# Softmax sums over a key tile and a sum of two tiles that GpSimd adds

## The chip, the cores and the metric

One core of a Trainium2 chip runs the whole program. The metric is the device time of one execution in microseconds. The kernel before took 1427.5 us (median of 3 runs, 1418.71 to 1435.67).

## The reference

A small network over eight sequences of 384 tokens, 512 wide: a state-space layer makes 256 tokens of each, 128 text tokens follow, then comes attention, then a mixture of 64 experts (6 for each token) with a shared expert. The change is in the attention, which is, for 16 query heads and 4 key heads of 32:

```python
x = layernorm(h)
q, k, v = heads(x @ Wq.T), heads(x @ Wk.T), heads(x @ Wv.T)
q = q * cos + rotate_half(q) * sin
k = k * cos + rotate_half(k) * sin
attn = softmax(q @ k.T * 32 ** -0.5)
h = h + (attn @ v) @ Wo.T
```

and, behind it, each token's six experts and its place in each expert's list, which the kernel works out while later sequences are in the attention:

```python
scores = softmax(x2 @ gate_w.T)
topk_w, topk_i = top_k(scores, 6)
pos = place_in_expert_list(topk_i)
```

## The kernel before, in words

The program has three stages: the state-space layer, the attention with the routing, and the experts. The attention is a software pipeline over passes b = -1 to 7. Pass b has 16 slots, n = 0 to 15, one for each query head of sequence b. In them the engines also prepare sequence a = b + 1 (normalise, transpose, project, rotate, transpose the heads, row maxima of the raw scores), project the output of c = b - 1, normalise and route d = b - 2, and place e = b - 3. Five engines run five instruction streams in the order in which the program is written, tied by semaphores. Nothing reorders them, so an instruction that waits holds up all that stands behind it on its engine.

A slot of the matrix engine (TensorE, PE) begins with the head's scores (L912): three matmuls, transposed, so that keys are on the partitions and the three key tiles of 128 keys by 384 queries lie in three PSUM banks. ScalarE takes the exponential of all three at once (L1171) into PT, a ring of eight heads in SBUF. The sums of the softmax and the products with the values are made by `values` (L916), for a group of four heads that share a key head, one group behind: in slots 4 to 7 for heads 0 to 3, and so on, the last group in slots 0 to 3 of the next pass. A step is one key tile for four heads, four matmuls with 32 columns of weights side by side. There are six: q = 0, 1, 2 multiply by ones (the sums), q = 3, 4, 5 by the values. `VALUE_STEPS` deals them to the four slots of a group as 2, 2, 1, 1. VectorE inverts the sums in the third slot of the group (L1421 to L1423) and multiplies at its end (L1431).

What else stands around the change:
- In slots 1, 2 and 4 PE projects the queries of sequence a, in slots 2, 3 and 5 its keys and values (L903). VectorE rotates each tile a slot later (L1387 to L1389), and GpSimd adds the two halves of the rotation (L1654, `rope_sum`) in slots 3, 4 and 6, into r1.
- In slot 7 PE transposes the heads out of r1 (L984). The first of these waits for the last `rope_sum`. ScalarE copies a rounded high part to qhi (L1278), VectorE the rest to qlo (L1395).
- SyncE copies qhi and qlo into the stacked operand QT of the scores, by `stack`: twelve transfers for eight heads, counted by stacked[half]. The half for heads 0 to 7 goes out at the end of pass b, that for heads 8 to 15 at the start of pass b + 1, behind `store_sums` (L806), which waits for the residual that VectorE makes in slot 0. Four small transfers (`stack_max`, L774) add the row maxima, counted by the same semaphore.
- The routing of sequence e: VectorE makes one-hot rows and a mask in slot 3 (L1466 to L1475), PE counts places in slot 4 (L1039), VectorE adds bases (L1487 to L1489), GpSimd adds the slot numbers and multiplies (L1663, L1665, three L1669, `places`), VectorE reduces that in slot 6 (L1495, `slots`), ahead of its last rotation. GpSimd scatters the result by 18 small DMAs (L1682) in slots 8 to 15.
- In slots 0, 1 and 5 GpSimd makes the low part of finished outputs (L1658, `out_lo`).

SBUF is nearly full: qhi, qlo, r1 and the normalised, transposed rows xT are parts of one arena, each free only between its last reader in one pass and its writer in the next.

## Time and profile before

| what | value |
|---|---|
| runs | 1418.71, 1427.5, 1435.67 us |
| profiled execution | 1441.19 us |
| its span, first to last instruction | 1439.4 us |
| mean granted TensorE clock | 0.945 of full |
| TensorE matmul busy | 1247.1 us (87%) |
| VectorE, ScalarE, GpSimd busy | 747.1, 417.8, 503.2 us (52%, 29%, 35%) |

The profile is of one execution. Times are microseconds from its first instruction. A row of the timeline gives start, duration, engine, line, operation, output from inputs, and in brackets how long the engine sat idle before it and what ended that.
### The profile page before, as it was taken

What the parts mean: (1) busy time and instruction counts of PE and PEld (TensorE: products, weight loads), DVE (VectorE), ACT (ScalarE), POOL (GpSimd) and SP (SyncE); (2) the same over time, 40 slices, a digit from 0 to 9 for tenths busy, and PEclk for the clock granted to TensorE, in tenths of its full rate; (3) what the DMA queues carried; (4) which work ended last, traced back from release to release, by engine and by line L of the source; (5) the groups of instructions that cost most, each with busy time, mean ns of one, the idle gap of its engine ahead of it and who ended that gap; (6) DMA issues with size and microseconds to landing.
All of it is one profiled execution on the core that took longest, in us unless ns stands there. A gap on an engine that the chain in (4) does not pass through costs nothing. (4 is left out here: it accounts for less than half of the span.)

```text
span 1439.4 us, 23556 instructions
## 1 busy us (share of the span) xinstructions
PE 1247.1 (87%) x9192; PEld 798.8 (55%) x9192; DVE 747.1 (52%) x1667; ACT 417.8 (29%) x693; POOL 503.2 (35%) x453
## 2 busy tenths in 40 slices
PE   6263778889999999999898789999999999989995
PEld 5253534445555554546455778666666666656662
DVE  7994457666677878686864532332322223222221
ACT  2220314344445444445354411111111111111110
POOL 0000101111114444443557673334444543444444
PEclk9698669999999999999999889999999999999997
DMA  3024142312525251615165263999999999998983
GB/s 115 0 62 101 39 89 42 86 42 64 129 63 134 53 144 43 155 35 136 46 198 181 97 195 53 290 309 295 303 336 341 299 337 343 282 299 284 331 271 40
DMA packets 144310, 239.82 MB, mean 167 GB/s; under 512 B 64569, under 2 KB 84681, under 8 KB 144201
## 3 DMA queue, kind: packets, MB, share of 16 engines
q1 hardware_dynamic: 120360, 214.10, 46.7%
q0 software_dynamic: 23840, 24.23, 9.4%
q8 instruction: 73, 1.20, 0.4%
q14 instruction: 37, 0.30, 0.1%
HBM read 175.59 MB, written 38.90 MB: 149 GB/s over the span
## 5 line engine op out<-in xcount | busy, mean ns | idle before, releaser
L2063 POOL DMA_INDIRECT out_rows<-mo_y,mo_scatter_half x128 | 182.9, 1429 | 239.8 <-DMA out_rows<-mo_y,mo_scatter_half 152.2
L1404 DVE TENSOR_REDUCE at_maxes<-at_ps 128x1 f32<-128x384 f32 x384 | 196.3, 553 | 59.5 <-PE at_ps L947 51.6
L1171 ACT ACTIVATE bulk<-at_ps 128x1152 f32<-128x1152 f32 x128 | 144.5, 1129 | 252.8 <-PE at_ps L912 251.5
L1682 POOL DMA_INDIRECT slot_table<-at_toki,at_si x144 | 145.5, 1011 | 119.9 <-DVE at_maxes L1404 87.0
L70 PE MATMUL mo_ps<-arena_view,arena_view 128*117 128x384 f32 (+1 forms) x864 | 168.8, 344 | 1.1 <-PEq L570 1.1
L70 PEld LDWEIGHTS mo_ps<-arena_view,arena_view 128*117 128x117 f32 (+1 forms) x864 | 146.5, 179 | 14.6 <-issue 14.5
L947 PE MATMUL at_ps<-late_view,late_view 128*128 128x384 bf16 x384 | 117.5, 352 | 28.9 <-DVE at_maxes L1404 16.7
L903 PE MATMUL at_ps<-arena_view,arena_view 128*128 128x512 f32 (+1 forms) x576 | 114.9, 351 | 3.6 <-ACT arena_view L1256 2.1
L903 PEld LDWEIGHTS at_ps<-arena_view,arena_view 128*128 128x128 f32 x576 | 90.6, 193 | 36.1 <-issue 22.3
L947 PEld LDWEIGHTS at_ps<-late_view,late_view 128*128 128x128 bf16 x384 | 31.0, 98 | 138.5 <-DVE at_maxes L1404 103.0
L912 PE MATMUL at_ps<-arena_view 97*128 97x384 f32 x384 | 96.4, 360 | 8.3 <-DMA arena_view<-at_mrow 5.1
L2038 DVE SCALAR_TENSOR_TENSOR mo_hm<-mo_sil,mo_wcol,mo_ps 128x352 f32<-128x352 f32 x32 | 18.6, 580 | 159.7 <-ACT mo_sil L1962 138.7
L903 PE MATMUL at_ps<-late_view,late_view 128*128 128x512 f32 x288 | 92.1, 436 | 6.1 <-POOL late_view L1658 4.3
L1658 POOL TENSOR_TENSOR late_view<-arena_view,late_view 128x384 fp32r<-128x384 f32 x32 | 32.0, 1012 | 160.8 <-ACT late_view L1233 160.8
L1908 PE MATMUL mo_ps<-late_view,mo_xgT 128*64 128x352 f32 x512 | 81.8, 474 | 5.7 <-DVE mo_xgT L2031 5.7
L1654 POOL TENSOR_TENSOR arena_view<-arena_view,arena_view 128x640 f32<-128x640 f32 x24 | 37.3, 1555 | 137.9 <-DVE arena_view L1389 137.9
L931 PE MATMUL at_ps<-bulk,at_ones 128*32 128x384 f32 x768 | 83.3, 513 | 1.3 <-ACT bulk L1171 0.8
L78 PE MATMUL mo_ps<-arena_view,arena_view 117*128 117x512 f32 (+1 forms) x324 | 78.9, 397 | 4.8 <-DVE arena_view L1995 4.8
L931 PE MATMUL at_ps<-bulk,arena_view 128*32 128x384 f32 x768 | 81.7, 499 | 0.0
L912 PEld LDWEIGHTS at_ps<-arena_view 97*128 97x128 f32 x384 | 67.9, 193 | 23.3 <-ACT bulk L1171 7.9
L1908 PE MATMUL mo_ps<-bulk,mo_xgT 128*64 128x352 f32 x512 | 79.3, 462 | 0.0
L78 PEld LDWEIGHTS mo_ps<-arena_view,arena_view 117*128 117x128 f32 (+1 forms) x324 | 59.6, 188 | 20.8 <-ACT arena_view L1950 5.5
(222 smaller groups left out, 1771.8 us busy)
## 6 DMA issues: line engine op xcount, KB each, us to landing
bulk<-in_L_ffn_w_gate SPq DMA_DIRECT2D x32, 704.0 KB
bulk<-in_L_ffn_w_up SPq DMA_DIRECT2D x32, 704.0 KB
late_view<-in_L_ffn_w_gate SPq DMA_DIRECT2D x32, 704.0 KB
late_view<-in_L_ffn_w_up SPq DMA_DIRECT2D x32, 704.0 KB
arena_view<-arena_view SPq DMA_DIRECT2D x96, 192.0 KB
late_view<-in_L_ffn_w_down SPq DMA_DIRECT2D x32, 512.0 KB
bulk<-in_L_ffn_w_down SPq DMA_DIRECT2D x32, 512.0 KB
out_rows<-at_hr SPq DMA_DIRECT2D x8, 768.0 KB
```

Source lines behind the costliest of these rows:

```text
L70: m = T.matmul(out, self.gu[:, wa, g, k, self.SO[c]:self.SO[c] + self.SW[c]], self.x2[:, xa, k, :], start=(n == 0), stop=(n == last))
L78: m = T.matmul(out, self.h[0:self.SW[c], xa, c, s * P:(s + 1) * P], self.d[0:self.SW[c], wa, c, :], start=(n == 0), stop=(n == last))
L903: m = T.matmul(out, xs[:, xa, k, x_cols], ws[:, wa, k, w_cols], start=(n == 0), stop=(n == 3 * KC - 1))
L912: m = T.matmul(ps[:, kt, 0:SEQ], QT[:, NH + h // REP, kt * P:(kt + 1) * P], QT[:, h, :], start=True, stop=True)
L931: m = T.matmul(ps[HD * j:HD * (j + 1), 3 + sums, 0:SEQ], w, PT[:, (REP * G + j) % RING, kt, :], start=(kt == 0), stop=(kt == NT - 1))
L947: T.matmul(ps[:, raw_bank(a, u), 0:SEQ], qb[:, r, s * P:(s + 1) * P], kb[:, g, :], start=True, stop=True).then_inc(raw_scores, 1)
L1171: A.activation(PT[:, N % RING, :, :], ps[:, 0:NT, 0:SEQ], ACT.Exp, scale=float(HD) ** -0.5)\
L1404: V.tensor_reduce(maxes[:, half, s, h:h + 1], ps[:, raw_bank(a, u), 0:SEQ], AX.X, ALU.max, negate=True)\
L1654: G.tensor_tensor(r1[:, s], r1[:, s], r2[:, s % 2], ALU.add).then_inc(rope_add, 1)
L1682: G.indirect_dma_start(slot_table, bass.IndirectOffsetOnAxis(ap=si[:, e % 2, m:m + 1], axis=0), toki[:, e % 2, m // TOPK:m // TOPK + 1], N ...
L1908: m = M.matmul(ps[CAP * e:CAP * (e + 1), 1 + g, 0:I], xgT[:, k, CAP * e:CAP * (e + 1)], wgu[j][:, e, g, k, :], start=(k == 0), stop=(k == ...
L2063: G.indirect_dma_start(acc_halves, bass.IndirectOffsetOnAxis(ap=scatter_half[:, half, 2 * p + e:2 * p + e + 1], axis=0), y[:, p % 2, e, co ...
```

## The change

For the seven sequences b = 0 to 6 (28 groups) GpSimd adds the exponentials of key tiles 0 and 1 of each head, 128x384 f32, as soon as they are there (`add_pair_of_tiles`), and the matrix engine multiplies tile 2 and this sum by ones: two sum steps in place of three. The five steps are dealt to the slots of a group as 2, 1, 1, 1. The last sequence keeps six steps.

The sums of the pairs need room, and there is no free buffer: they lie over qlo (heads 0 to 3), the high half of xT (heads 4 to 7), its low half (heads 8 to 11) and r1 (heads 12 to 15). So the first addition of each four waits until what lies there has been read: the stack of heads 8 to 15, the last projections, or the transposes of the heads. The next writers of these buffers wait for the sums of that group. The row maxima get a semaphore of their own, so that GpSimd can wait for the stack alone.

```diff
@@ attention_phase, tables @@
+        max_stacked = [sem(f"max_stacked{i}") for i in range(2)]
+        pair_added = sem("pair_added")
...
-        VALUE_STEPS = {0: (0, 1), 1: (2, 3), 2: (4,), 3: (5,)}
+        VALUE_STEPS = {0: (0, 1), 1: (2,), 2: (3,), 3: (4,)}
+        LAST_STEPS = {0: (0, 1), 1: (2, 3), 2: (4,), 3: (5,)}
+        ADDED = NKV * (B - 1)
+
+        def sum_steps(G):
+            return NT - 1 if G < ADDED else NT
...
-        STACK = 16 * (2 * 6 + P // HD)
+        STACK = 16 * 2 * 6
+        MAX_STACK = 16 * (P // HD)
+        PAIR_SUM = [part(arena, (15872, 6144, 7680, 10752)[g], [REP, SEQ]) for g in range(NKV)]
@@ SyncE @@
-                                 .bitcast(F32), mrow[HD * j:HD * j + NH // 2, half, :, :]).then_inc(stacked[half], 16)
+                                 .bitcast(F32), mrow[HD * j:HD * j + NH // 2, half, :, :]).then_inc(max_stacked[half], 16)
...
+                sp.wait_ge(sums_done, NKV * (B - 1))
@@ TensorE @@
                 if h in (0, NH // 2):
                     pe.wait_ge(stacked[2 * h // NH], STACK * (b + 1))
+                    pe.wait_ge(max_stacked[2 * h // NH], MAX_STACK * (b + 1))
...
-                kt, sums = q % NT, 1 - q // NT
+                first = sum_steps(G)
+                kt, sums = (q, 1) if q < first else (q - first, 0)
+                if first < NT and sums:
+                    kt = NT - 1 - q
...
-                if q == NT:
+                if q == 1 and G < ADDED:
+                    pe.wait_ge(pair_added, REP * (G + 1))
+                if q == first:
...
-                    m = T.matmul(ps[HD * j:HD * (j + 1), 3 + sums, 0:SEQ], w, PT[:, (REP * G + j) % RING, kt, :],
-                                 start=(kt == 0), stop=(kt == NT - 1))
-                if q == NT - 1:
+                    added = q == 1 and G < ADDED
+                    probs = PAIR_SUM[g][:, j, :] if added else PT[:, (REP * G + j) % RING, kt, :]
+                    m = T.matmul(ps[HD * j:HD * (j + 1), 3 + sums, 0:SEQ], w, probs,
+                                 start=q in (0, first), stop=q in (first - 1, first + NT - 1))
+                if q == first - 1:
...
-                    G, steps = NKV * b + n // REP - 1, VALUE_STEPS[n % REP]
+                    G = NKV * b + n // REP - 1
+                    steps = (VALUE_STEPS if G < ADDED else LAST_STEPS)[n % REP]
@@ ScalarE @@
+                        wait(act, sums_done, NKV * (b - 1) + 3)
@@ VectorE: rope, q_lo, max_row @@
+                if s == 0:
+                    wait(dve, sums_done, NKV * (a - 1))
...
+                if i == 0 and a >= 1:
+                    dve.wait_ge(sums_done, NKV * (a - 1) + 1)
...
-                    dve.wait_ge(stacked[half], STACK * a)
+                    dve.wait_ge(max_stacked[half], MAX_STACK * a)
@@ GpSimd @@
+            def add_pair_of_tiles(b, n):
+                g, N = n // REP, NH * b + n
+                if n % REP == 0:
+                    if g == 0:
+                        pool.wait_ge(stacked[1], STACK * (b + 1))
+                    elif g in (1, 2):
+                        pool.wait_ge(q_ready, NT * (b + 2))
+                        pool.wait_ge(kv_ready, NT * (b + 2))
+                    else:
+                        pool.wait_ge(heads_turned, NTILE * (b + 2))
+                pool.wait_ge(probs_ready, N + 1)
+                G.tensor_tensor(PAIR_SUM[g][:, n % REP, :], PT[:, N % RING, 0, :], PT[:, N % RING, 1, :],
+                                ALU.add).then_inc(pair_added, 1)
...
                     if nxt and n - 1 in KV_SLOT:
                         rope_sum(a, KV_SLOT[n - 1])
+                    if main and n != 0 and b < B - 1:
+                        add_pair_of_tiles(b, n)
                     if nxt and a + 1 < B and n == 7:
                         inverse_deviation(a + 1)
                     if prev3 and n == 4:
...
                     if prev2 and n == 0:
                         inverse_deviation2(d)
+                    if main and n == 0 and b < B - 1:
+                        add_pair_of_tiles(b, n)
```

What this does to the order of the instructions is shown at three places, in a pass in which all five sequences are in work (b = 4). The first is GpSimd's queue at the start of a pass, slots 0 to 3. Before (late_view_1738 is the output's low part, arena_view_1739 is r1):

```order
L1658 TENSOR_TENSOR late_view_1738<-arena_view_1748,late_view_1738 128x384 [waits at_ohi_ready] x2
L1675 TENSOR_TENSOR at_rstd<-at_ve,at_mhalf 128x3 [waits at_var2_ready]
L1677 TENSOR_TENSOR at_shift<-at_shift,at_rstd 128x3 [waits at_rstd_step2]
L1658 TENSOR_TENSOR late_view_1738<-arena_view_1748,late_view_1738 128x384 [waits at_ohi_ready]
L1654 TENSOR_TENSOR arena_view_1739<-arena_view_1739,arena_view_1740 128x640 [waits at_rope_k,at_rope_q] x2
```

After, with lines moved down by the diff (L1691 is the addition, L1696 `out_lo`, L1678 `rope_sum`; arena_view_1753 is the pair sum of heads 0 to 3, in qlo):

```order
L1696 TENSOR_TENSOR late_view_1738<-arena_view_1748,late_view_1738 128x384 [waits at_ohi_ready] x2
L1713 TENSOR_TENSOR at_rstd<-at_ve,at_mhalf 128x3 [waits at_var2_ready]
L1715 TENSOR_TENSOR at_shift<-at_shift,at_rstd 128x3 [waits at_rstd_step2]
L1691 TENSOR_TENSOR arena_view_1753<-bulk 128x384 [waits at_probs_ready,at_stacked1]
L1696 TENSOR_TENSOR late_view_1738<-arena_view_1748,late_view_1738 128x384 [waits at_ohi_ready]
L1691 TENSOR_TENSOR arena_view_1753<-bulk 128x384 [waits at_probs_ready] x2
L1678 TENSOR_TENSOR arena_view_1739<-arena_view_1739,arena_view_1740 128x640 [waits at_rope_k,at_rope_q]
L1691 TENSOR_TENSOR arena_view_1753<-bulk 128x384 [waits at_probs_ready]
L1678 TENSOR_TENSOR arena_view_1739<-arena_view_1739,arena_view_1740 128x640 [waits at_rope_k,at_rope_q]
```

The addition for head 0, with its wait for the stack, stands ahead of an `out_lo` and of both first rotation sums.

The second is GpSimd's queue in slots 4 to 7. Before, the places of sequence e (late_view_1750), an `out_lo` and the last rotation sum:

```order
L1663 TENSOR_TENSOR late_view_1750<-late_view_1750,at_slot 128x192 [waits at_place_ready]
L1665 TENSOR_TENSOR late_view_1750<-late_view_1750,at_lg 128x192 [waits at_slot_step]
L1669 TENSOR_TENSOR at_hv<-at_hot,late_view_1750 128x384 [waits at_slot_step]
L1669 TENSOR_TENSOR at_hv<-at_hot,late_view_1750 128x384 x2
L1658 TENSOR_TENSOR late_view_1738<-arena_view_1748,late_view_1738 128x384 [waits at_ohi_ready]
L1654 TENSOR_TENSOR arena_view_1739<-arena_view_1739,arena_view_1740 128x640 [waits at_rope_k,at_rope_q]
L1647 TENSOR_TENSOR at_rstd<-at_ve,at_mhalf 128x3 [waits at_var_ready]
```

After, from the addition for head 4 on (arena_view_1754 is the pair sum of heads 4 to 7, in the high half of xT):

```order
L1691 TENSOR_TENSOR arena_view_1754<-bulk 128x384 [waits at_probs_ready,at_kv_ready,at_q_ready]
L1701 TENSOR_TENSOR late_view_1750<-late_view_1750,at_slot 128x192 [waits at_place_ready]
L1703 TENSOR_TENSOR late_view_1750<-late_view_1750,at_lg 128x192 [waits at_slot_step]
L1707 TENSOR_TENSOR at_hv<-at_hot,late_view_1750 128x384 [waits at_slot_step]
L1707 TENSOR_TENSOR at_hv<-at_hot,late_view_1750 128x384 x2
L1696 TENSOR_TENSOR late_view_1738<-arena_view_1748,late_view_1738 128x384 [waits at_ohi_ready]
L1691 TENSOR_TENSOR arena_view_1754<-bulk 128x384 [waits at_probs_ready]
L1678 TENSOR_TENSOR arena_view_1739<-arena_view_1739,arena_view_1740 128x640 [waits at_rope_k,at_rope_q]
L1691 TENSOR_TENSOR arena_view_1754<-bulk 128x384 [waits at_probs_ready] x2
L1671 TENSOR_TENSOR at_rstd<-at_ve,at_mhalf 128x3 [waits at_var_ready]
```

The addition for head 4, with its wait for the projections, stands ahead of the places, and that for head 5 ahead of the last rotation sum.

The third is TensorE in slots 4 and 5, the steps of heads 0 to 3. Before (L931 with at_ones is a sum step, with arena_view_1745 a value step, L903 a projection):

```order
L931 MATMUL at_ps<-bulk,at_ones 32x384 [waits at_divide_step,at_probs_ready]
L931 MATMUL at_ps<-bulk,at_ones 32x384 x3
L1039 MATMUL at_ps<-at_mask,at_upper 128x64 [waits at_x2T_ready,at_pos_read,at_mask_ready]
L1039 MATMUL at_ps<-at_mask,at_upper 128x64 x8
L931 MATMUL at_ps<-bulk,at_ones 32x384 x4
L903 MATMUL at_ps<-arena_view_65,arena_view_1737 128x512 [waits at_rope_q,at_xlo_ready,at_xhi_ready]
L903 MATMUL at_ps<-arena_view_65,arena_view_1737 128x512 x11
L912 MATMUL at_ps<-arena_view_1746 128x384 [waits at_probs_ready]
L912 MATMUL at_ps<-arena_view_1746 128x384 x2
L931 MATMUL at_ps<-bulk,at_ones 32x384 x4
L931 MATMUL at_ps<-bulk,arena_view_1745 32x384 [waits at_o_ready,at_v_copied]
L931 MATMUL at_ps<-bulk,arena_view_1745 32x384 x3
```

After (L949 is the same line, L913 the projection):

```order
L949 MATMUL at_ps<-bulk,at_ones 32x384 [waits at_divide_step,at_probs_ready]
L949 MATMUL at_ps<-bulk,at_ones 32x384 x3
L1057 MATMUL at_ps<-at_mask,at_upper 128x64 [waits at_x2T_ready,at_pos_read,at_mask_ready]
L1057 MATMUL at_ps<-at_mask,at_upper 128x64 x8
L949 MATMUL at_ps<-arena_view_1753,at_ones 32x384 [waits at_pair_added]
L949 MATMUL at_ps<-arena_view_1753,at_ones 32x384 x3
L913 MATMUL at_ps<-arena_view_65,arena_view_1737 128x512 [waits at_rope_q,at_xlo_ready,at_xhi_ready]
L913 MATMUL at_ps<-arena_view_65,arena_view_1737 128x512 x11
L923 MATMUL at_ps<-arena_view_1746 128x384 [waits at_probs_ready]
L923 MATMUL at_ps<-arena_view_1746 128x384 x2
L949 MATMUL at_ps<-bulk,arena_view_1745 32x384 [waits at_o_ready,at_v_copied]
L949 MATMUL at_ps<-bulk,arena_view_1745 32x384 x3
```

The second sum step of slot 4 waits for the additions, and the sum step of slot 5 is gone.

## Rows read from the trace of the kernel before

**Rows 1.** Page, part 2: tenths of each of 40 equal slices of the span

```profile
PE   6263778889999999999898789999999999989995
...
PEclk9698669999999999999999889999999999999997
```

**Rows 2.** SyncE's timeline, pass b = 4: start us, duration us, engine, line, operation, xcount

```profile
495.54 3.18 SPq L765 DMA_DIRECT2D arena_view<-arena_view  x3
...
503.02 2.15 SPq L768 DMA_DIRECT2D arena_view<-arena_view  x3
```

**Rows 3.** Windows: us, busy of each engine, PEclk, DMA share, GB/s

```profile
505.00:506.00 1.00, 1.00 (x8) 0.78 (x6) 0.63 (x2) 0.30 (x1) 0.00 (x0) 1.00 0.60 137
506.00:507.00 1.00, 0.94 (x9) 0.47 (x11) 1.00 (x4) 0.91 (x2) 0.00 (x0) 1.00 0.06 14
```

**Rows 4.** Merged timeline of pass b = 4, slots 3 to 7

```profile
506.29 1.13 ACT L1171 ACTIVATE bulk<-at_ps 128x1152 f32<-128x1152 f32 x1
...
506.64 1.49 DVE L1466 TENSOR_TENSOR at_hot<-at_iota,at_mf 128x384 bf16<-128x384 f32 x3
...
508.16 0.46 DVE L1473 TENSOR_TENSOR at_threes<-at_hot 128x576 bf16<-128x576 bf16 x1
...
511.33 0.85 PE L931 MATMUL at_ps<-bulk,at_ones 128*32 128x384 f32 x8
...
513.04 0.61 POOL L1663 TENSOR_TENSOR late_view<-late_view,at_slot 128x192 f32<-128x192 f32 x1 [1.21 <-DVE at_lg L1488]
...
514.40 2.69 POOL L1669 TENSOR_TENSOR at_hv<-at_hot,late_view 128x384 f32<-128x384 bf16 x3
...
515.58 0.85 PE L931 MATMUL at_ps<-bulk,at_ones 128*32 128x384 f32 x8
...
516.25 0.83 PE L931 MATMUL at_ps<-bulk,arena_view 128*32 128x384 f32 x8
...
517.01 1.69 PE L903 MATMUL at_ps<-arena_view,arena_view 128*128 128x256 f32 x12
517.13 1.35 DVE L1495 TENSOR_REDUCE at_sf<-at_hv 128x18 f32<-128x1152 f32 x1 [0.61 <-POOL at_hv L1669]
...
519.21 0.29 DVE L1387 TENSOR_TENSOR arena_view<-at_ps,at_cos 128x128 f32<-128x128 f32 x1 [0.24 <-DVE at_tokf L1499]
...
519.91 1.55 POOL L1654 TENSOR_TENSOR arena_view<-arena_view,arena_view 128x640 f32<-128x640 f32 x1 [1.52 <-DVE arena_view L1389]
...
523.25 1.15 PE L984 MATMUL at_ps<-late_view,arena_view 128*128 128x128 f32 x9
```

**Rows 5.** Timeline, GpSimd and VectorE, passes b = 4 and b = 7

```profile
498.70 1.02 POOL L1658 TENSOR_TENSOR late_view<-arena_view,late_view 128x384 fp32r<-128x384 f32 x1
498.71 1.04 DVE L1463 CAST at_mf<-at_mi 128x24 f32<-128x24 uint32 x1
...
736.74 0.18 DVE L1463 CAST at_mf<-at_mi 128x24 f32<-128x24 uint32 x1
...
747.24 3.34 POOL L1669 TENSOR_TENSOR at_hv<-at_hot,late_view 128x384 f32<-128x384 bf16 x3
```

**Rows 6.** Instructions of L1510: xcount, duration ns min/median/max

```profile
L1510 DVE TENSOR_TENSOR arena_view<-arena_view,arena_view x14: 684/887/1670, 738.0 to 818.4; 128x704 fp32r<-128x704 f32 x8, 117x512 fp32r<-117x512 f32 x4, 118x512 fp32r<-118x512 f32 x2
```

**Rows 7.** TensorE's timeline, first pass (b = 0)

```profile
250.53 0.88 PE L947 MATMUL at_ps<-late_view,late_view 128*128 128x384 bf16 x2 [1.19 <-DVE at_maxes L1404]
251.34 1.51 PE L931 MATMUL at_ps<-bulk,arena_view 128*32 128x384 f32 x8
```

**Rows 8.** Windows of the first pass, columns as in rows 3

```profile
246.00:252.00 6.00, 4.14 (x25) 1.39 (x26) 5.44 (x11) 3.44 (x5) 0.00 (x0) 0.90 0.01 3
252.00:258.00 6.00, 5.67 (x27) 1.68 (x19) 3.82 (x9) 1.13 (x1) 0.00 (x0) 0.54 0.01 1
```

**Rows 9.** Timeline of pass b = 1, slots 5 to 7

```profile
297.77 1.69 PE L903 MATMUL at_ps<-arena_view,arena_view 128*128 128x256 f32 x12
...
301.89 1.15 PE L984 MATMUL at_ps<-late_view,arena_view 128*128 128x128 f32 x9
```

2 lines of the change are left out of this document (1 added, 1 removed).

## The prediction

> **What bounds the kernel now.** I read the page's slices first: in the stretch of the attention, after the first quarter of the span, the matrix engine is busy in nine tenths of every slice and its granted clock stands near full [rows 1]. Then, since the change makes the matrix engine wait for GpSimd, I read SyncE's timeline for the copies that GpSimd will stand behind [rows 2, 3], and the merged timeline of one pass through the middle of the attention (b = 4, from 489 us on) [rows 4]. The reader is to see there that the matrix engine goes from one head to the next without a gap, so that a matmul taken out of it is time gained, and that GpSimd has idle stretches but sits in two handovers: the sum of the rotated halves (L1654), which releases the transposes of the heads (L984), and the slot products (L1669), for which VectorE waits at L1495.
>
> **What is removed.** One step of four matmuls for each of 28 groups of heads (seven sequences of four). The third sum step at 515.58 is followed by a value step 0.67 us later [rows 4], and 0.67 is what a step costs at full clock. 28 x 0.67 = 18.8 us. I count 25 of them, 17 us: in the first pass the matrix engine already waits for row maxima (1.19 us at 250.53) [rows 7], so that two there hide, and one falls into the last pass, which waits for weights. Bounds 15 and 19.
>
> **What is added on GpSimd.** 112 additions of 128x384 f32 from two SBUF inputs. L1658 is the same form, 1.02 us [rows 5]; I take 1.01, since two in a row come sooner. 16 of them are 16 us in each pass, and GpSimd, busy for 35% of the span, has the room. The cost is in where they stand, since GpSimd works its queue in order.
>
> **First wait, the pair sum of heads 0 to 3.** The addition for head 0 writes over the low halves of the queries (qlo), so it waits for the stack of heads 8 to 15 to be copied out. SyncE issues these twelve transfers behind the store of an earlier sequence's rows, which waits for a residual of slot 0 (`store_sums`, then `stack`). So the first goes out at 495.54 and the last has been issued at 505.17 [rows 2]. The DMA engines are 0.60 busy in the microsecond after 505 and 0.06 in the next [rows 3], so I take 506.2 for the landing. Before, only head 8's scores needed this copy, in the slot after the transposes of 523.25 [rows 4], and it was covered. Now GpSimd stands at it, and behind it in the queue are the low half of an output, two rotation sums and the other additions. Up to head 3's addition that is four operations of 1.01, one of 1.55 and one of 1.01: 506.2 + 6.6 = 512.8. The exponentials of head 3 are done at 507.4 [rows 4]. The matrix engine is at its second sum step at 511.33, and 0.67 earlier with slot 1 lightened: 510.66. It waits 2.2 us with the handover. The first two passes send their stack early, without that store; the other five with additions (b = 2 to 6) pay: 5 x 2.2 = 11 us, and 1.3 more in b = 6, whose copies go out later relative to its start. If the copy landed as its last issue ends, the wait would be 1 us; if a microsecond later, 3.2. Bounds 5 and 16.
>
> **Second wait, the transposes of the heads in slot 7.** The addition for head 4 writes over the high half of the normalised rows (xT) and waits for the last key and value projection, in slot 5. In GpSimd's queue the places of an earlier sequence, which before ran at 513.04, stand behind that addition. The chain is then, from the end of the projection (517.01 + 1.69 = 518.70 before): addition 1.01; places, 513.04 to 517.09, 4.05; VectorE's slots and what follows until its rotation begins, 517.13 to 519.21, 2.08; the rotation until GpSimd's sum begins, 0.70; that sum 1.55 [rows 4]. Together 9.4, with handovers 9.5. The low half and head 5's addition fit beside VectorE's part. Before, the matrix engine came to the transposes on its own at 523.25, 4.55 after the projection. So it will wait 5.0 us. This holds where a place computation and an addition meet, b = 3 to 6: 4 x 5.0 = 20 us. In b = 1 there are no places, and the queue is addition, low half, addition, sum: 4.6 us against the 2.4 from 299.46 to 301.89 [rows 9], 2.2 us; in b = 0 without the low half 1.2. In b = 2 the logits on the matrix engine cover it. Sum 23.4. Bounds 20 and 28: the upper one if VectorE's statistics, which are now late too and stand ahead of the low halves of the queries, add another 1 us in each of four passes.
>
> **VectorE beside the additions.** A CAST of 24 columns takes 0.18 us alone and 1.04 where an L1658 starts beside it; three slot products take 3.34 instead of 2.69 [rows 4, 5] where VectorE has a subtraction with two SBUF inputs, whose own time runs from the median 887 ns to 1670 [rows 6]. In slots 3 and 4 of b = 3 to 6 the routing's six two-input operations will meet the six queued operations of GpSimd; in slot 6 two casts meet an addition. At 0.65 for three, 1.3 and 0.85: 2.15 x 4 = 8.6 us. Bounds 0 (they miss each other) and 14 (the 0.65 twice as often). The Trainium skill, "SBUF — State Buffer", section "Who interferes with whom", says more than these rows: an instruction with two SBUF inputs on VectorE and one that reads SBUF on GpSimd exclude each other for their whole length. By that at least the four longest of the six (1.49 and 0.46 [rows 4]) would stand in GpSimd's chain in full, and the term would be 4 x (1.95 + 0.85) = 11 or more instead of 8.6.
>
> **The clock.** In the first pass, after a wait of 1.19 us [rows 7] and thin work, the granted clock falls to its lower level: its mean is 0.90 from 246 to 252 and 0.54 from 252 to 258 [rows 8], which is 1.2 + 5.5 = 6.7 us at half. A sum or value step in it takes 1.51 instead of 0.85 [rows 7, 4]. So such a stretch costs at most 3.3 us. The four waits of 5 us will surely be followed by such a stretch, but there the engine is paced by ScalarE and VectorE in part: 2 us each. The five of 2.2 us sometimes: 0.4 each. Sum 10. Bounds 0 and 30 (nine times 3.3).
>
> **Hidden.** The additions of heads 8 to 15 come 1 us after their exponentials and are wanted a slot or more later; the scatters that they push back are waited for a pass later. The other new waits (for sums long done) cost nothing. After the attention everything moves as one: the experts' loads start at its last value step.
>
> **Sum.** -17 + 11 + 1.3 + 23.4 + 8.6 + 10 = +37 us. Against the profiled execution of 1441.2 that is 1478; it was 13.7 above the median of the runs shown, 1427.5, to which I add the same: 1464.5.
>
> **Rivals.**
> 1. The additions are ready in time and the matrix engine stays the bound: the other side. It speaks for it that an addition takes 1 us and GpSimd has idle time. It needs the copy to land before 504, so that head 3's addition is done by 510.6, and the projection of slot 5 to release its addition without the places behind it. The first is against the issue times, the second against the queue's order. From there on it gives -17: 1410.5.
> 2. Gain and waits cancel: only the four waits in slot 7 are long, the copy lands with its last issue and neither clock nor ports cost much. -17 + 20 + 5 = +8: 1436.
> 3. The waits are as above, but the clock stays up and VectorE is not held: -17 + 11 + 1.3 + 23.4 = +19: 1446.
> 4. Every wait costs a full stretch at half clock, and the ports the full 14: 19 + 30 + 14 = +63: 1490.
>
> **How the numbers follow.** A measurement of this kernel can tell about 1%, 14 us, from no change. Forecast (both waits, with some loss by clock and ports) 0.45; rival 3 0.27; rival 4 0.12; rival 2 0.10; rival 1 0.06. Faster by over 1% is rival 1: 0.06. Within 1% is rival 2: 0.10. Slower is the rest, 0.84. The range leaves out rival 1, rival 2 and the far end of rival 4: 1441 to 1486.
>
> **What would show it right or wrong.** In the profile after: the matrix engine idle some 2 us ahead of the second sum step of slot 4 in five passes, released by GpSimd's addition; idle some 5 us ahead of the transposes of slot 7 in four passes, released by the rotation sum; the first addition of a pass starting with the end of the stack's copies; VectorE's slot reduction starting 8 us later after its slot began; a dip of the granted clock after these waits; passes b = 3 to 6 about 9 us longer than before, passes 0 and 1 about as long as before. The prediction fails if the first addition starts in slot 1, if the transposes of slot 7 don't wait, or if the passes b = 3 to 6 are shorter than before.

## The result and the profile after

| | before | after |
|---|---|---|
| median of the runs | 1427.58 us (1418.71 to 1435.67) | 1467.93 us (1465.61 to 1472.72) |
| ratio | 1 | 1.0287, 95% interval 1.0237 to 1.0337 |
| profiled execution, its span | 1441.19, 1439.4 us | 1472.72, 1470.6 us |
| mean granted TensorE clock | 0.945 | 0.928 |
| GpSimd busy | 503.2 us | 614.0 us |

The changed kernel is slower by 40 us, 3.4 us beyond the predicted 1464.5. Some executions take over 1.5% longer than the fastest of their kernel; medians here are of all runs, ratios leave such executions out. The page of the changed kernel, parts 1 and 5, shows that an addition takes as long as it was said to take:

```profile
PE 1245.7 (85%) x8968; PEld 804.2 (55%) x8968; DVE 767.7 (52%) x1667; ACT 418.7 (28%) x693; POOL 614.0 (42%) x565
...
L1691 POOL TENSOR_TENSOR arena_view<-bulk 128x384 f32<-128x384 f32 x112 | 113.0, 1014 | 237.6 <-ACT bulk L1190 118.2
```

112 additions of 1.014 us (1.01 was taken from [rows 5]) keep GpSimd busy for 113.0 us; it is busier by 110.8. TensorE has 112 matmuls less (224 recorded instructions), but its busy time barely moves from 1247.1, because others ran longer at the lower clock: the transposes of the heads take 23.1 us in all instead of 18.3, the projections of 512 columns from the arena 82.4 instead of 75.5.

To see where the time went I use one measure throughout: a pass of the attention, from the start of its first exponential on ScalarE to that of the next. Two rows of ScalarE's timeline bound passes 1 to 6, the first exponentials of pass 1 and of pass 7:

```profile
272.67 1.13 ACT L1190 ACTIVATE bulk<-at_ps 128x1152 f32<-128x1152 f32 x1 [4.08 <-PE at_ps L923]
...
748.09 1.13 ACT L1190 ACTIVATE bulk<-at_ps 128x1152 f32<-128x1152 f32 x1 [3.70 <-issue]
```

Between them lie 475.4 us; before it was 440.4. The same reading of both kernels, pass by pass (us):

| kernel | b = 0 | 1 | 2 | 3 | 4 | 5 | 6 | 1 to 6 |
|---|---|---|---|---|---|---|---|---|
| before | 76.3 | 70.4 | 73.4 | 73.9 | 73.9 | 73.9 | 74.9 | 440.4 |
| after | 76.6 | 69.0 | 73.4 | 83.7 | 82.2 | 83.8 | 83.3 | 475.4 |

Passes 3 to 6 carry the whole loss, 36.4 us; pass 1 gains 1.4. A second profile of each kernel tells what such a reading is worth.

> The kernel before, profiled once more, to see which readings repeat. Passes 1 to 6 together were 440.4 us, pass 0 76.3, all outside the seven passes 922.7. If the passes are a steady reading: 438 to 441 again, while pass 0 and what lies outside move by several us. If the first profile's execution, which was 13.7 us above the median, was long in the passes: below 436, and the steps taken out are worth less than 0.66 us each.

> The changed kernel, profiled once more. Passes 1 to 6 together were 475.4 us, pass 0 76.6, all outside the seven passes 918.6. If the passes are a steady reading: 473 to 478 again, and about 35 above the second profile of the kernel before. If the clock's falls differ much from execution to execution: off by more than 5.

Measured: passes 1 to 6 took 440.5 and 475.1 us, within 0.3 of the first profiles. Pass 0 took 72.6 and 74.0, in place of 76.3 and 76.6, and the rest of the span moved by up to 10 us. So passes 1 to 6 are a steadier measure than the time of a run, and pass 0 is left out below. Two repeats don't show the whole spread, however. The kernel with both waits filled (under "TensorE kept busy in the waits") runs the same instructions in passes 1 and 2 as the change, and these two took 3.8 us more there. A window over slot 7 of pass 1 (us, busy of PE, PEld, DVE, ACT and POOL, granted clock, DMA share, GB/s), first in the changed kernel, then in that one, shows the granted clock at 1.00 and at 0.60, with the same 27 matmuls:

```profile
301.01:307.30 6.29, 3.66 (x27) 2.29 (x27) 4.29 (x12) 4.56 (x9) 4.80 (x6) 1.00 0.01 4
...
295.79:304.33 8.54, 6.40 (x27) 4.08 (x27) 4.51 (x12) 4.92 (x9) 4.79 (x6) 0.60 0.00 1
```

Ahead of that slot's transposes TensorE waits 2.07 us in both. So the same wait is followed by a fall of the clock in one execution and not in another, and a difference of passes between two single profiles can be off by some 4 us.

Now the merged timeline of the changed kernel, pass b = 4, slots 3 to 7 (start, duration, idle time before and its releaser in brackets), the counterpart of [rows 4]:

```profile
514.57 2.30 DVE L1490 TENSOR_TENSOR at_hot<-at_iota,at_mf 128x384 bf16<-128x384 f32 x3
...
515.10 1.34 POOL L1691 TENSOR_TENSOR arena_view<-bulk 128x384 f32<-128x384 f32 x1 [7.75 <-DMA arena_view<-arena_view]
...
516.90 1.16 DVE L1497 TENSOR_TENSOR at_threes<-at_hot 128x576 bf16<-128x576 bf16 x1
...
518.09 0.95 DVE L1498 TENSOR_TENSOR at_mask<-at_threes 128x192 bf16<-128x192 bf16 x1
...
520.07 0.44 PE L1057 MATMUL at_ps<-at_mask,at_upper 128*128 128x64 bf16 x9 [1.12 <-DVE at_mask L1499]
...
521.06 2.87 DVE L1505 TENSOR_SCALAR late_view<-late_view,at_rsum 128x64 f32<-128x64 f32 x3
521.37 0.99 POOL L1691 TENSOR_TENSOR arena_view<-bulk 128x384 f32<-128x384 f32 x1
...
522.41 0.85 PE L949 MATMUL at_ps<-arena_view,at_ones 128*32 128x384 f32 x8 [1.91 <-POOL arena_view L1691]
...
523.20 4.62 PE L913 MATMUL at_ps<-arena_view,arena_view 128*128 128x512 f32 x12
...
529.05 1.69 PE L913 MATMUL at_ps<-arena_view,arena_view 128*128 128x256 f32 x12
...
530.89 1.01 POOL L1691 TENSOR_TENSOR arena_view<-bulk 128x384 f32<-128x384 f32 x1 [7.02 <-issue]
...
531.85 0.59 POOL L1701 TENSOR_TENSOR late_view<-late_view,at_slot 128x192 f32<-128x192 f32 x1
...
533.18 2.67 POOL L1707 TENSOR_TENSOR at_hv<-at_hot,late_view 128x384 f32<-128x384 bf16 x3
...
535.89 1.35 DVE L1519 TENSOR_REDUCE at_sf<-at_hv 128x18 f32<-128x1152 f32 x1 [6.68 <-POOL at_hv L1707]
...
539.00 1.54 POOL L1678 TENSOR_TENSOR arena_view<-arena_view,arena_view 128x640 f32<-128x640 f32 x1 [1.25 <-DVE arena_view L1411]
...
540.64 2.15 PE L1002 MATMUL at_ps<-late_view,arena_view 128*128 128x128 f32 x9 [5.19 <-POOL arena_view L1678]
```

Read it from the wait backwards. At 522.41 TensorE is let go by head 3's addition (521.37), the last of a queue that could not begin before 515.10, when the stack's copy had landed: the first wait. At 540.64 it is let go by a rotation sum; ahead of that sum stands the chain of the addition for head 4 (530.89, as soon as the projection of 529.05 ends), the places and slot products, then VectorE's reduction and the last rotation: the second wait. Beside the queued additions VectorE's small operations are long (0.95 us for a mask addition), and TensorE meets that too, at 520.07. The granted clock falls after both: the projection at 523.20 takes 4.62 us, and the transposes 2.15 instead of 1.15 [rows 4]. The view of waits sums the three over the kernel (line, awaited line, us in all, times, longest):

```profile
PE at_ps L1002 <- POOL arena_view L1678: 23.1, 5, 5.2
...
PE at_ps L949 <- POOL arena_view L1691: 12.1, 5, 2.9
PE at_ps L1057 <- DVE at_mask L1499: 10.2, 6, 3.7
```

Of the third row only 3.1 us, in four waits, lie in passes 3 to 6. The other two waits, 3.4 and 3.7 us, come at 828.3 and 859.0, behind the last pass, where nothing is added; two of 3.3 and 2.6 us stand there before the change too.

### The profile page after: what moved, and what is told of

Same layout as the page of the kernel before. It is cut to its first block and busy times, and to the rows that moved or that the text cites. A ratio compares the mean times of both kernels' runs of the same rounds, so it can differ in the third digit from the quotient of the medians.

```text
span 1470.6 us, 23258 instructions
## 1 busy us (share of the span) xinstructions
PE 1245.7 (85%) x8968; PEld 804.2 (55%) x8968; DVE 767.7 (52%) x1667; ACT 418.7 (28%) x693; POOL 614.0 (42%) x565
## 3 DMA queue, kind: packets, MB, share of 16 engines
q8 instruction: 72, 1.18, 0.3%
## 5 line engine op out<-in xcount | busy, mean ns | idle before, releaser
L1691 POOL TENSOR_TENSOR arena_view<-bulk 128x384 f32<-128x384 f32 x112 | 113.0, 1014 | 237.6 <-ACT bulk L1190 118.2
L913 PE MATMUL at_ps<-arena_view,arena_view 128*128 128x512 f32 (+1 forms) x576 | 121.8, 365 | 3.6 <-ACT arena_view L1275 2.1
L913 PEld LDWEIGHTS at_ps<-arena_view,arena_view 128*128 128x128 f32 x576 | 95.7, 202 | 39.2 <-issue 23.8
L2080 DVE SCALAR_TENSOR_TENSOR mo_hm<-mo_sil,mo_wcol,mo_ps 128x352 f32<-128x352 f32 x32 | 18.6, 581 | 158.8 <-ACT mo_sil L2004 144.0
L913 PE MATMUL at_ps<-late_view,late_view 128*128 128x512 f32 x288 | 91.7, 435 | 6.3 <-POOL late_view L1696 4.2
L949 PE MATMUL at_ps<-bulk,arena_view 128*32 128x384 f32 x768 | 86.4, 526 | 0.0
L913 PEld LDWEIGHTS at_ps<-late_view,late_view 128*128 128x128 f32 x288 | 52.5, 194 | 20.7 <-issue 13.3
L2004 ACT ACTIVATE mo_sil<-mo_ps 128x352 f32<-128x352 f32 x32 | 14.9, 464 | 166.6 <-PE mo_ps L1950 159.1
```

The lines of the kernel that those rows point to most:

```text
L913: m = T.matmul(out, xs[:, xa, k, x_cols], ws[:, wa, k, w_cols], start=(n == 0), stop=(n == 3 * KC - 1))
L949: m = T.matmul(ps[HD * j:HD * (j + 1), 3 + sums, 0:SEQ], w, probs, start=q in (0, first), stop=q in (first - 1, first + NT - 1))
L1691: G.tensor_tensor(PAIR_SUM[g][:, n % REP, :], PT[:, N % RING, 0, :], PT[:, N % RING, 1, :], ALU.add).then_inc(pair_added, 1)
```

## The experiments

All are edits of the changed kernel, so line numbers shift a little from one to the next; ratios stand against the kernel before on the same chip, and each kernel's passes are those of one profiled execution.

**No additions.** What are the removed steps worth alone?

```diff
-                if q == 1 and G < ADDED:
-                    pe.wait_ge(pair_added, REP * (G + 1))
...
-                    added = q == 1 and G < ADDED
+                    added = False
...
-                    if main and n != 0 and b < B - 1:
-                        add_pair_of_tiles(b, n)
...
-                    if main and n == 0 and b < B - 1:
-                        add_pair_of_tiles(b, n)
```

> The change without its additions: GpSimd adds nothing, nobody waits for a pair sum, and the second sum step multiplies key tile 1 alone (tile 0 is left out of the softmax sums). Queue order elsewhere is that of the change. Theory (the matrix engine is the bound, and all the loss comes from the additions in GpSimd's queue): the kernel before less 17 us, about 1410 us (1407 to 1414), passes 2.5 to 2.8 us shorter than before, no wait ahead of the transposes of slot 7. Rival (the steps taken out were hidden, the gain does not exist): within 5 us of the kernel before, about 1427.

Measured: 1415.62 us, ratio 0.9882 (0.9825 to 0.994); passes 1 to 6 424.5 us. The timed value is 2 us above the expected span; the passes give 440.4 - 424.5 = 15.9 us for 24 steps, 0.66 each, close to the 0.67 read from [rows 4]. The first term of the sum holds. Single passes are 1.9 to 3.8 us shorter (expected 2.5 to 2.8). VectorE's timeline of this kernel also shows the routing with GpSimd quiet, for comparison below:

```profile
490.51 1.49 DVE L1488 TENSOR_TENSOR at_hot<-at_iota,at_mf 128x384 bf16<-128x384 f32 x3
492.03 0.46 DVE L1495 TENSOR_TENSOR at_threes<-at_hot 128x576 bf16<-128x576 bf16 x1
492.52 0.26 DVE L1496 TENSOR_TENSOR at_mask<-at_threes 128x192 bf16<-128x192 bf16 x1
...
495.36 0.72 DVE L1503 TENSOR_SCALAR late_view<-late_view,at_rsum 128x64 f32<-128x64 f32 x3
```

**Additions of heads 4 and 5 behind the last rotation sum.** This undoes the second wait alone.

```diff
+        ADD_SLOT = {1: (1,), 2: (2,), 3: (3,), 6: (4, 5, 6), 7: (7,)}
...
-                    if main and n != 0 and b < B - 1:
-                        add_pair_of_tiles(b, n)
+                    for m in ADD_SLOT.get(n, (n,) if n > 7 else ()) if main and b < B - 1 else ():
+                        add_pair_of_tiles(b, m)
```

> The change with the additions of heads 4 and 5 moved behind the last rotation sum in GpSimd's queue, so that the places and that sum no longer stand behind the wait for the projections. The first wait stays. Theory (order of the queue): the wait of 5.2 us ahead of the transposes of slot 7 in passes 3 to 6 and the short ones in passes 0 and 1 go, with the dip of the clock behind them: 4 x (5 + 1 to 2) + 3 = 27 to 31 us less than the change, about 1439. Rival (the work itself: 112 additions and the ports they share with VectorE cost the time wherever they stand): less than 8 us from the change, 1460 or more.

Measured: 1449.36 us, ratio 1.0133 (1.0073 to 1.0193), 18.6 below the changed kernel; passes 1 to 6 447.3 us, 28.1 less. The passes are as expected (27 to 31), the timed fall is not. In the timeline the transposes no longer wait for a rotation sum, and slots 6 and 7 of pass 4 are back at 4.19 and 4.78 us (7.97 and 7.21 with the change). Slot 4 of pass 4 keeps its length, 9.20 us (9.38). In passes 5 and 6 it is 1.7 and 2.7 us shorter and in pass 2 1.4 longer, with the same wait and another granted clock (1.00 in passes 5 and 6, where it was 0.82 and 0.67). So some 25 of the 28.1 us belong to the second wait. The waits of this kernel have the first one untouched and of the second nothing (the 2.4 us left stand ahead of the first pass, and did so before the change):

```profile
PE at_ps L950 <- POOL arena_view L1692: 12.1, 5, 2.9
PE at_ps L1003 <- POOL arena_view L1679: 2.4, 1, 2.4
```

So the second wait comes from the order of GpSimd's queue, not from too little room on it.

**Heads 0 to 3 behind the first rotation sum.** This shortens the queue ahead of the rotation sum but leaves the late buffer.

```diff
+        ADD_SLOT = {3: (0, 1, 2, 3), 4: (4,), 5: (5,), 6: (6,), 7: (7,)}
...
-                    if main and n == 0 and b < B - 1:
-                        add_pair_of_tiles(b, n)
```

The loop over `ADD_SLOT` stands here, and in the three kernels that have this table below, as in the experiment before.

> The change with the additions of heads 0 to 3 put together behind the first rotation sum, so that an output's low part and that sum no longer stand behind the wait for the stack; the second wait stays. Theory: head 3's addition then ends about when the matrix engine comes to it, so that the wait of 1.9 us ahead of the second sum step of slot 4 and the dip of the clock in the projection behind it (1.6 us) shrink in passes 2 to 6; VectorE's one-hot operations may still be held by the additions beside them: 8 to 18 us less than the change, about 1455. Rival (the work itself): less than 5 us from the change.

Measured: 1461.41 us, ratio 1.0201 (1.0137 to 1.0265), 6.5 below the changed kernel by the time and 17.9 by passes 1 to 6 (457.5); expected were 8 to 18, so that the time alone would have missed. Slot 4 falls to 5.3 to 5.8 us. GpSimd's timeline, pass 4, shows why so much of the first wait went:

```profile
505.93 1.56 POOL L1679 TENSOR_TENSOR arena_view<-arena_view,arena_view 128x640 f32<-128x640 f32 x1 [3.52 <-DVE arena_view L1412]
509.39 4.61 POOL L1692 TENSOR_TENSOR arena_view<-bulk 128x384 f32<-128x384 f32 x4 [1.90 <-DMA arena_view<-arena_view]
515.19 1.57 POOL L1679 TENSOR_TENSOR arena_view<-arena_view,arena_view 128x640 f32<-128x640 f32 x1 [1.19 <-DVE arena_view L1412]
```

The four additions still wait for the copy (509.39), but an output's low half and a rotation sum no longer stand between them. The late copy alone leaves TensorE 1.4 us of waits for pair sums in passes 2 to 6; the copy with six operations queued behind it makes the 12.1.

**Both moves.**

```diff
+        ADD_SLOT = {3: (0, 1, 2, 3), 6: (4, 5, 6), 7: (7,)}
```

> Both moves together: the additions of heads 0 to 3 behind the first rotation sum, those of heads 4 to 6 behind the last. The same 112 additions and the same five steps on the matrix engine. Theory: nearly the whole gain of the steps comes out, less 0 to 8 us for VectorE held by additions in slots 3 and 4: 1410 to 1420, about 1415, faster than the kernel before. Rival (the work itself): still slower than the kernel before, 1440 or more.

Measured: 1432.85 us over all ten runs, 1422.7 over the seven that the ratio counts, 0.9975 (0.9922 to 1.0028); passes 1 to 6 432.9 us. Either median is above the 1410 to 1420 expected: 8.5 us of the passes are left over the kernel without additions, although TensorE waits for pair sums for only 2.4 us in the whole kernel. The next two runs split the remainder.

**Additions that nobody reads.** The same additions at the same places, with their reader taken away; once with both moves, once with the change's own order.

```diff
-                if q == 1 and G < ADDED:
+                if q == first + NT - 1 and G < ADDED:
                     pe.wait_ge(pair_added, REP * (G + 1))
...
-                    added = q == 1 and G < ADDED
+                    added = False
...
-                        wait(act, sums_done, NKV * (b - 1) + 3)
+                        wait(act, pair_added, REP * (NKV * (b - 1) + 3))
```

The other waits that keep a pair sum's buffer from being written over are changed from `sums_done` to `pair_added` in the same way.

> As the run with both moves (heads 0 to 3 behind the first rotation sum, heads 4 and 5 behind the last), but no step reads the pair sums: the second sum step reads key tile 1 alone, and TensorE asks for the pair sums only at the last value step. Only the additions' use of GpSimd and of the memory is left. It splits what was left of that run over the kernel without additions (1432.9 against 1415.6; 509 against 497 us over the seven passes). If the additions slow VectorE and that is what is left: 1428 to 1433 us, passes together 506 to 509. If it is TensorE waiting in slot 4 for the pair sum: 1415 to 1418, passes 497 to 499.

Measured: 1431.49 us, ratio 0.9973 (0.9935 to 1.0012); passes 1 to 6 431.4 us. Only 1.5 us of the remainder was waiting for pair sums, which is within the spread of such a difference; 6.9 us is there without any wait for them. VectorE, GpSimd and TensorE in pass 4 of this kernel show what it is:

```profile
497.01 4.74 POOL L1692 TENSOR_TENSOR arena_view<-bulk 128x384 f32<-128x384 f32 x4 [1.76 <-DMA arena_view<-arena_view]
498.76 1.16 DVE L1498 TENSOR_TENSOR at_threes<-at_hot 128x576 bf16<-128x576 bf16 x1
499.94 0.95 DVE L1499 TENSOR_TENSOR at_mask<-at_threes 128x192 bf16<-128x192 bf16 x1
500.93 0.94 DVE L1500 TENSOR_TENSOR at_mask<-at_mask,at_threes 128x192 bf16<-128x192 bf16 x1
...
502.91 1.97 DVE L1506 TENSOR_SCALAR late_view<-late_view,at_rsum 128x64 f32<-128x64 f32 x3
...
514.22 1.17 PE L1003 MATMUL at_ps<-late_view,arena_view 128*128 128x128 f32 x9 [0.49 <-issue]
...
517.19 1.01 PE L1003 MATMUL at_ps<-late_view,arena_view 128*128 128x128 f32 x6 [1.01 <-DVE arena_view L1420]
```

The three mask operations take 3.05 us, with GpSimd quiet 0.46 + 0.26 + 0.26, and each is about as long as one of the additions beside it; those take 1.19 instead of 1.01. TensorE waits 1.12 us for that mask in this pass. Behind it the routing's tail is late: in slot 7 TensorE stands 0.49 us ahead of the first transposes (514.22; the last rotation sum ends at 514.12) and 1.01 us ahead of the second lot for VectorE's low halves (517.19), for which it waits 0.58 without additions.

> The change with its 112 additions where it has them, in the same order on GpSimd, but the second step of a sum reads key tile 1 alone in place of the pair sum (tile 0 is left out of the sums), and TensorE asks for the pair sums only at the last value step, three slots later. So the first wait is gone; the rotation sums still stand behind the additions (second wait), and the additions still share the memory with VectorE. Theory, three causes side by side: slot 4 falls from 9.4-10.8 to 5.0-5.5 us in passes 3 to 6 (the mask additions on VectorE stay slow), slots 6 and 7 stay at about 8.0 and 7.2; some 16-20 us less than the changed kernel, 1448 to 1452 us. Rival, slot 4 is late through the mask on VectorE alone and the pair sums are awaited by no one: 1464 to 1468. Rival, the pair-sum wait delays everything behind it and the second wait exists only because of the first: below 1435.

Measured: 1457.0 us, ratio 1.0193 (1.0126 to 1.0261), above the 1448 to 1452 expected; passes 1 to 6 456.4 us, 19.0 below the changed kernel, as expected (16 to 20), though the timed fall is only 11. Slot 4 of passes 3 to 6 is 5.0 to 5.8 us, slots 6 and 7 stay at 8.0 and 7.3 to 7.8. The waits of this kernel hold the rotation sum's row unchanged, and no row for the pair sums:

```profile
PE at_ps L1002 <- POOL arena_view L1678: 23.1, 5, 5.2
...
PE at_ps L1057 <- DVE at_mask L1499: 8.0, 6, 2.7
```

Taking the first wait away leaves the second as it was, and the experiment that took the second away left the first's 12.1 us: the two are independent.

**TensorE kept busy in the waits.** What does the clock cost by itself? Useless matmuls fill the second wait, and in a second kernel both.

```diff
+                    if nxt and n == 7 and prev3:
+                        pe.wait_ge(rope_q, NT * (a + 1))
+                        for _ in range(18):
+                            T.matmul(ps[:, 5, :], WxT[:, 0, 0, 0:P], WxT[:, 0, 0, 0:512], start=True, stop=True)
                     if nxt and n == 7:
                         turn_heads(a, 0)
```

> The change as it is, and 18 matmuls of 512 columns with no use, which TensorE runs in the four passes with a long second wait, behind the last rotation and ahead of slot 7's transposes. They fill the idle time; nothing waits less. If the clock's fall after that wait costs time of its own (slot 8's matmuls took 2.15 us for 1.15): the granted clock of slots 7 and 8 stays high, and the time is 6 to 10 us less than the changed kernel, 1458 to 1462. If the clock costs nothing on the path: 1468 within 3. If the filling itself outlasts the wait: up to 1475.

Measured: 1471.9 us, ratio 1.0288 (1.0218 to 1.0357), no less than the changed kernel; passes 1 to 6 471.0 us, 4.4 less. TensorE's timeline of pass 4:

```profile
529.34 4.26 PE L1111 MATMUL at_ps<-arena_view 128*128 128x512 f32 x18
534.74 1.17 PE L1002 MATMUL at_ps<-late_view,arena_view 128*128 128x128 f32 x9 [1.15 <-POOL arena_view L1682]
535.85 0.85 PE L949 MATMUL at_ps<-bulk,arena_view 128*32 128x384 f32 x8
537.71 1.01 PE L1002 MATMUL at_ps<-late_view,arena_view 128*128 128x128 f32 x6 [1.01 <-DVE arena_view L1423]
```

The clock did stay up (transposes 1.17 us, not 2.15), but the gain was handed on: TensorE now stands 1.01 us at VectorE's low halves (0.56 before the change). Slot 7 went from 7.2-7.9 to 5.6-6.8, 3.7 us over four passes, where I expected 6 to 10.

> The change as it is, with TensorE kept busy in both waits: the 18 useless matmuls ahead of slot 7's transposes as before, and in slot 4 of the same four passes 5 ahead of the places and 8 ahead of the second sum step. Filling the second wait held the clock there (0.50 to 1.00) and gave back 0.4 to 1.6 us in a pass, because VectorE's low halves came next; in slot 4 nothing but TensorE's own projection stands behind the wait. If the fall of the clock is priced in slot 4: its projection goes from 4.62 back to 3.0 us, slot 4 from 9.3-10.7 to 7.7-9.1, and the time is 6 us below the run with one wait filled, about 1465. If the clock costs nothing there either: slot 4 stays at 9.3 to 10.7 and the time at 1472.

Measured: 1460.91 us, ratio 1.0212 (1.0135 to 1.0288), 4 below the 1465 expected; passes 1 to 6 468.5 us, with the 3.8 us in passes 1 and 2 that were told above. Windows of the changed kernel in pass 4, just after its first and its second wait (us, busy of PE, PEld, DVE, ACT and POOL, granted clock, DMA share, GB/s):

```profile
522.80:525.80 3.00, 3.00 (x15) 2.10 (x8) 1.88 (x4) 0.00 (x0) 1.07 (x1) 0.62 1.14 366
...
540.80:543.80 3.00, 3.00 (x17) 1.79 (x16) 2.86 (x10) 1.87 (x4) 2.66 (x4) 0.50 0.00 0
```

The same two places in the kernel with both waits filled:

```profile
518.80:521.80 3.00, 3.00 (x19) 2.13 (x12) 1.92 (x4) 0.00 (x0) 1.12 (x1) 1.00 1.12 359
...
533.80:536.80 3.00, 1.85 (x18) 1.12 (x17) 2.90 (x10) 2.27 (x5) 3.00 (x3) 1.00 0.00 0
```

And its projection of slot 4 in TensorE's timeline:

```profile
519.25 3.02 PE L913 MATMUL at_ps<-arena_view,arena_view 128*128 128x512 f32 x12
```

The clock is 1.00 where it was 0.62 and 0.50, and the projection takes 3.02 us instead of 4.62. Slot 4 of passes 3 to 6 fell from 9.4-10.8 to 7.8-8.1, 8.6 us together (7.2 and 8.1 against the two other profiles in which this wait isn't filled): here nothing but TensorE's own projection stands behind the wait, and the clock is paid in full.

**Another buffer and other places.** Can the removed steps be kept without the waits? The pair sums of heads 0 to 3 go into the residual's rows, which stand empty then:

```diff
-        PAIR_SUM = [part(arena, (15872, 6144, 7680, 10752)[g], [REP, SEQ]) for g in range(NKV)]
+        ADD_SLOT = {1: (), 2: (0, 1, 2), 3: (3,)}
+        PAIR_SUM = [hr[:].rearrange("p s d -> p (s d)").rearrange("p (r q) -> p r q", r=REP)] + \
+            [part(arena, n, [REP, SEQ]) for n in (6144, 7680, 10752)]
...
+                    if b < B - 1:
+                        sp.wait_ge(sums_done, NKV * b + 1)
                     rows_in(hr, c, r_in)
...
-                        pool.wait_ge(stacked[1], STACK * (b + 1))
+                        wait(pool, h2_stored, 16 * (b - 1))
+                        wait(pool, x2_ready, NT * (b - 1))
...
                         inverse_deviation(a + 1)
+                    if main and n == 7 and b < B - 1:
+                        for m in range(4, 8):
+                            add_pair_of_tiles(b, m)
```

> Both waits taken away with the change's arithmetic whole: the pair sums of heads 0 to 3 go into the rows buffer of the residual, which stands empty until slot 5 or so, so that they needn't wait for the end of the stack's copy; heads 0 to 2 are added in slot 2, head 3 in slot 3, heads 4 to 7 in slot 7 behind the inverse deviation, and the residual's rows are loaded behind the sums of heads 0 to 3. Theory (order on GpSimd and the late buffer make the waits): within 5 us of the kernel without additions, 1414 to 1421 us, faster than both kernels. Rival, the additions slow VectorE wherever they stand: no better than the run with both moves, 1428 to 1435. Rival, the later load of the residual's rows delays the output projection's residual: slots 11 to 15 longer, above 1435.

> The kernel of the run with the pair sums in the rows buffer, once more, to narrow its interval against the kernel before. Its seven passes together were 500.8 us against 516.7 before and 496.9 without additions. If the passes decide: 1.0% under the kernel before, ratio 0.988 to 0.992. If the first run's ratio of 0.995 was the true size, with half of the gain lost outside the passes: 0.994 to 0.997.

Measured: 1424.5 us, ratio 0.995 (0.9914 to 0.9987), and again 1424.75, ratio 0.996 (0.9928 to 0.9992): below both kernels, though by only half a per cent of the kernel before. Passes 1 to 6 take 425.4 and 426.3 us, within 2 of the kernel without any additions. The timeline of pass 4 shows where the additions went, and what VectorE's mask costs beside them:

```profile
488.58 2.97 POOL L1696 TENSOR_TENSOR at_hr<-bulk 128x384 f32<-128x384 f32 x3 [1.42 <-issue]
...
494.25 1.05 POOL L1696 TENSOR_TENSOR at_hr<-bulk 128x384 f32<-128x384 f32 x1 [1.19 <-ACT bulk L1194]
495.74 0.46 DVE L1501 TENSOR_TENSOR at_threes<-at_hot 128x576 bf16<-128x576 bf16 x1
496.24 0.26 DVE L1502 TENSOR_TENSOR at_mask<-at_threes 128x192 bf16<-128x192 bf16 x1
...
510.93 3.88 POOL L1696 TENSOR_TENSOR arena_view<-bulk 128x384 f32<-128x384 f32 x4
```

All 112 additions are there, and the mask is back at 0.46 and 0.26. In slot 2 and late in slot 7 VectorE mostly reads PSUM: its low halves, with one input in PSUM and one in SBUF, take 1.49 us for three beside the additions of 510.93, as without additions. TensorE's slots 4 to 7 are as long as in the kernel without additions. The run changes the buffer and the places at once and doesn't tell what each is worth.

The time missed the 1414 to 1421 expected, and of the two cases set out for the second run the worse one came, in which half of the gain is lost: the passes fell by 14 to 15 us, the time by 6 to 7 by the ratios. Measured against the kernel before, the times of the kernels with additions lie some 1 to 15 us above what passes 1 to 6 say, that of the kernel without additions 3. The profiles don't show where: outside passes 0 to 6 they have 909 to 925 us with additions and 913 to 923 without. A profile is one execution, that of the kernel with heads 4 and 5 moved is 11 us shorter than its median, and the cause stays open.

## Why the prediction was right

The chain of kernels gives each term as a difference of passes 1 to 6 (pass 0's share, one step and 1.2 us of the second wait, is taken off the forecast):

| term | forecast | measured | from |
|---|---|---|---|
| steps removed, 24 of them | -16.1 | -15.9 | no additions, 424.5, less before, 440.4 |
| VectorE beside the additions | 8.6 | 6.9 | both moves, unread, 431.4, less no additions |
| second wait, with its clock | 22.2 + 8 | 25.0 | change, unread, 456.4, less both moves, unread |
| first wait, with its clock | 12.3 + 2 | 19.0 | the change, 475.4, less change, unread |
| sum | 37 | 35.0 | |

Differences along one chain add up of themselves. Each has the spread of some 4 us shown above, and VectorE's is measured at the moved places: at the change's own, slot 4 of passes 3 to 6 holds 3.3 us of it, there 2.1, and the 1.2 us between them stand in the row of the second wait.

- **Steps removed.** 0.66 us for each step, taken as 0.67.
- **First wait.** The view of waits has 12.1 us in five waits for the pair sums, the longest 2.9 (forecast 11 + 1.3 us in five, 2.2 each and 1.3 more in b = 6). That the sum agrees so well is partly luck: pass 6 has 1.9, not 3.5, and passes 2, 3 and 5 have 2.6 to 2.9. In pass 4 the copy landed 16.3 us after the pass's first exponential (forecast 16.0: the 506.2 worked out from [rows 2, 3] less the 490.2 at which pass 4 then began; in passes 3 and 5 it was 17.2); head 3's addition was done 0.95 us later in the pass than computed, 0.3 by the copy, the rest because the operations beside VectorE took up to 1.34 us instead of 1.01.
- **Second wait.** 23.1 us in five, the longest 5.2, of which 2.4 stand ahead of the first pass as before: 20.7 for the four (forecast 5.0 each). Pass 1 has 2.07 us (forecast 2.2) and pass 0 1.18 (1.2), by TensorE's rows of L1002; the view doesn't name GpSimd as their releaser. From the end of the projection to the transposes it took 540.64 - 530.74 = 9.9 us, forecast 9.5. Pass 2 was spared, as said.
- **VectorE held.** 1.6 us on average in passes 3 to 6 (292.7 for 286.1 us), forecast 2.15. The mechanism was the one named. What I had not listed is a wait that it makes by itself: TensorE stands at the late mask, 3.1 us in four waits of passes 3 to 6, where there is none without additions. In the change most of this hides under the first wait, which ends later.
- **The clock.** The sum was near, 12.3 us against 10, but the split behind it was off. I gave 8 us to the long second waits and 2 to the short first ones ("sometimes: 0.4 each"). Measured with TensorE kept busy it was 3.7 and 8.6. The step that failed is the price of a single fall. At the long waits, where ScalarE and VectorE were already said to pace the engine in part, 2 us each came to 0.9, since VectorE's low halves come next there. At the short ones 0.4 us each came to 2.1 in passes 3 to 6, since TensorE's own projection stands behind them. What counted was who stood behind the wait, more than its length. "Sometimes" was right: of the short waits in slot 4 that of pass 2 (2.56 us) left the clock at 1.00, those of passes 3 to 6 a mean over the slot of 0.67 to 0.82.

The Trainium skill, "SBUF — State Buffer", section "Who interferes with whom", has a two-input operation of VectorE and one of GpSimd that reads SBUF shut each other out. The rows of the unread additions agree: 0.26 becomes 0.95, the length of an addition. By that rule the prediction would have had the term at 11 or more in place of its 8.6, and 6.9 was measured: perhaps because part of what VectorE lost lay off TensorE's path, which no run tells apart.

Rival 1 (the additions ready in time) is what the kernel with another buffer then did: it took two other places and a buffer that is free early, not more speed of GpSimd. Rival 2 (four waits only, no price for clock and VectorE) and rival 3 (waits alone) are refuted by the unread additions and by the kernels whose waits are filled, rival 4 by the clock's 12.3 us.

The median rose by 40.4 us while the passes rose by 35.0. The prediction carried the profiled execution's 13.7 us over the median to the kernel after, whose own was 4.8 above its median; this is chance between executions: the second profile of the kernel before is 13.5 us shorter with the same passes 1 to 6. That the median came out 3.4 us from the forecast is therefore in part luck.

## What to carry to other kernels

An operation moved to an engine with idle time costs what stands behind it in that engine's queue: look for the last thing its first input or its buffer waits for, and count every operation of other work that the wait will now hold back. Choose a place beside work of the neighbour engine that the operation doesn't hold up, and a buffer that is free early; the same 112 additions cost 51 us in the passes with one set of places and buffers and under 2 with another. Price a fall of the clock by whether the matmuls after it or another engine decide what comes next.

## What the runs showed of the hardware

Not expected were two things. VectorE's scaling of the gate scores (L1505), which has one tensor input and a scalar for each partition, is held by GpSimd as well: three take 0.72 us alone, 1.97 beside a rotation sum and 2.87 beside one of the change's additions and a rotation sum; the prediction counted operations with two inputs and casts, but not this one. The same section of the Trainium skill's page "SBUF — State Buffer" names such an operation among those that can contend with GpSimd for the shared ports, and the rows agree. And matmuls without any use, 18 in a wait of 5 us, kept the granted clock at 1.00 where it had been 0.50, as the windows of the experiment show.
